# A CIN and MLP tower on one core: the 320-wide sum over d as two matmuls on 64 rows each, into two PSUM banks

## The chip, the cores and the metric

The kernel runs on one core of a Trainium2 chip. The metric is the device time of one execution in microseconds (us), as the median of several runs. One further execution was taken by the hardware profiler, and all rows below come from it.

## What is computed

For 1024 samples, 39 embedding rows of 16 numbers are gathered from 39 tables, giving `e` (sample b, field f, component d). Three cross layers follow, and then a three-layer MLP:

```python
x0 = xk = e                                   # (b, 39, 16)
for W in (f0, f1, f2):
    z = einsum('bfd,bgd->bfgd', x0, xk).reshape(b, f * g, d)
    xk = einsum('bpd,pm->bmd', z, W)          # (b, 128, 16)
    outs.append(xk)
z = concatenate(outs, axis=1).sum(-1)         # sum over d: (b, 384)
h = relu(concatenate([z, dense_ctx], 1) @ W_top1 + b_top1)
y = relu(h @ W_top2 + b_top2) @ W_top3
```

Since only the sum over d of the third layer is wanted, the kernel never forms it for each d. It forms, for each sample, field f and channel g, the sum over d of x0[f, d] * x2[g, d], called s3, and then multiplies it by f2.

## The kernel before

All arithmetic is fp32; where it matters, a product is split by hand into a high and a low part (fp32r) and made in three matmul passes. A batch is 128 samples (8 batches), a batch has 4 groups of 512 columns (32 samples times 16 values of d), and a group has 4 tiles of 128 columns, which are 8 samples times 16 values of d. A tile is a step `u`: 16 steps per batch. Each engine has its own program of the same loop: two steps ahead, then a hardware loop over batches with `u` from 2 to 17, then the last batch and a tail. Nothing but this hand-written order and the semaphores sets the order of the work.

**One step on TensorE** (`step`, `cin2`). For the second layer, a step goes through 10 banks `q` of four fields each (the last has three). For each bank TensorE makes three passes of 512 columns (lines 456, 457, 460) into one of a ring of five PSUM banks, 0 to 4. ScalarE (line 664, banks 0, 3, 5, 7) and VectorE (line 809, the other six banks) multiply each field's 128 columns by the tile's scalars x0 and add into `terms`; GpSimd adds the terms up (lines 351, 355) into `x2`, which holds the 128 columns of the tile two steps back in its partitions and 128 channels as columns.

**The sum over d** (`sum_s3`, line 470). In bank position `q == 5` (`S3_AT`) of each step from `u = 2`, TensorE multiplies `x2` as the stationary operand by `x0_diag`, a block-diagonal matrix of 8 samples times 40 columns (39 fields and a column of ones), which is 320 columns, into PSUM bank 5. ScalarE's `store_s3` (line 676) copies these to `s3` at bank position 6. There are 128 such sums. `x0_diag` is filled by eight DMAs for each group (`move_diag`), one for each sample's 16 rows; its zeros and ones are set once, in the prologue of VectorE.

**The rest of the PSUM.** Bank 6 (`X1_BANK`) takes the first layer's sum. Bank 7 (`MISC_BANK`) is shared in time by the turned scalars (`turn_scalars`, line 416: four transposes of 39x39, in tile 1 at bank position 0), the turned inputs of the next batch (`turn`, line 404, four transposes at each of four places `TURNS`, each stored by ScalarE's `store_cols`, line 616), and the third layer's matmuls `cin3` (line 480), stored by `store_r`.

**The first layer** (`cin1`, line 435). It is interleaved into tiles 1, 2 and 3 at the seven places `CIN1`; the first, in tile 1 at bank position 6, waits for the group's products, which VectorE makes (line 781) in tiles 0 and 1.

**The tail.** The last two sums, then the MLP in fp32: `layer1` (line 545), which begins each of its banks with a matmul of 16 rows (`wt1_dense`), `layer2` (555), `cin3` (480), `layer3` (562).

Of the kernel before, what the change touches and what calls it, by code (L numbers as in the profile page):

```python
# [33 lines left out]
P = 128  # L34
B, F, D, G = 1024, 39, 16, 128
# [3 lines left out]
TILES = 4  # L39
# [21 lines left out]
CHAINS = 2  # L61
TERMS = NA * FB
W1_CHUNKS = 3
S3_BANK, X1_BANK, MISC_BANK = 5, 6, 7
SPLIT = (0, 1, 2)
NS = len(SPLIT)
CIN1_ORDER = (0, 1, 3, 4, 5, 6, 2)
# [7 lines left out]
CIN1 = ((1, 6), (1, 9), (2, 2), (2, 5), (2, 8), (3, 1), (3, 4))  # L75
STORE_X1, SPLIT_X1 = (3, 4), (3, 5)
CIN3 = (7, 8, 9)
L1_BANKS = ((6, 0, 1, 2), (3, 4, 0, 1))
L2_BANKS = ((6, 2), (3, 4))
L3_BANKS = (5, 2)  # L80

ROWS_AT = (9, 3)
TURNS = ((9, 7), (10, 0), (10, 4), (10, 8))
TREE = (8, 4, 2)

def layout_constants():

    mask = (np.arange(P)[:, None] // D == np.arange(TB)[None, :]).astype(np.float32)
    return mask, np.eye(P, dtype=np.float32)  # L90

# [8 lines left out]
def cin_tower(nc, dense_ctx, ids, tables, w_top1, b_top1, w_top2, b_top2, w_top3,  # L101
              w0_pair, w0_mirror, f1, f2, c_mask, c_eye, out):
    with ExitStack() as ctx:
# [10 lines left out]
        w0 = sb("w0", [KR, KT, G])  # L114
        w0_high = sb("w0_high", [KR, NS, G], F32R)
        w0_low = sb("w0_low", [KR, NS, G], F32R)
        mask = sb("mask", [P, TB])
        eye = sb("eye", [P, P])
        ids_now = sb("ids_now", [P, F], U32)
        x0_in = sb("x0_in", [P, F, D])  # L120
# [6 lines left out]
        x1_high = sb("x1_high", [P, 2, GCOLS], F32R)  # L127
        x1_low = sb("x1_low", [P, 2, GCOLS], F32R)
        x0_scal = sb("x0_scal", [P, 2, TILES, F])
        x0_diag = sb("x0_diag", [P, 2, TILES, TB, FX])  # L130
        terms = sb("terms", [P, 2, TERMS, G])
        x2 = sb("x2", [P, 2, G])
        s3 = sb("s3", [P, FX, BATCH])
# [112 lines left out]
        @block.sync  # L246
        def _(sp):
            sp.dma_start(ids_now[:, :], ids[0:BATCH, :].bitcast(U32)).then_inc(s_ids, 16)
            sp.dma_start(w0_a.rearrange("r (k m) -> r k m", m=G), w0_pair.rearrange("k r m -> r k m")) \
                .then_inc(s_w0, 16)  # L250
            sp.dma_start(w0_b.rearrange("r (k m) -> r k m", m=G), w0_mirror.rearrange("k r m -> r k m")) \
                .then_inc(s_w0, 16)
            f1_v = f1.rearrange("(f g) m -> g f m", g=G)
            n = F // W1_CHUNKS
            for c in range(W1_CHUNKS):
                sp.dma_start(w1_raw[:, c * n * G:(c + 1) * n * G].rearrange("p (f m) -> p f m", m=G),
                             f1_v[:, c * n:(c + 1) * n, :]).then_inc(s_w1[c], 16)
            sp.dma_start(w2[:, :, :], f2.rearrange("(f g) m -> g f m", g=G)).then_inc(s_w2, 16)

            def load_ids(bt):  # L260
                sp.wait_ge(s_gather, bt * (16 * F))
                sp.dma_start(ids_now[:, :], ids[bass.ds(bt * BATCH, BATCH), :].bitcast(U32)) \
                    .then_inc(s_ids, 16)

            def move_first(j):

                at = j % GROUPS * GCOLS
                for i in range(SPT):
                    row = -KT * i % F
                    sp.dma_start(x0_first[i * F:(i + 1) * F, j % 2, :], x0_cols[row:row + F, at:at + GCOLS]) \  # L270
                        .then_inc(s_first[j % 2], 16)

            def move_diag(gf, j):

                sp.wait_ge(s_scal, gf + 1)
                sp.wait_ge(s_s3, gf * TILES - TILES + CREDIT_S3)
                for b in range(TB):
                    rows = slice(b * D, (b + 1) * D)
                    sp.dma_start(x0_diag[rows, j % 2, :, b, 0:F], x0_scal[rows, j % 2, :, :]) \
                        .then_inc(s_diag[j % 2], 16)  # L280

            def move(gf, j):

                if j > 0:

                    sp.wait_ge(s_x1, gf)
                if j % GROUPS == 0:
                    move_first(j)
                at = j % GROUPS * GCOLS  # L290
                for k in range(1, KT):
                    sp.dma_start(prods[0:KR, k, :], x0_cols[k:k + KR, at:at + GCOLS]).then_inc(s_second[k - 1], 16)
                if j == 0:
                    sp.wait_ge(s_cols, 4)
                if j % GROUPS < GROUPS - 1:
                    move_first(j + 1)

            load_ids(1)
            sp.wait_ge(s_cols, 1)
            move(0, 0)  # L300
            sp.wait_ge(s_ones, 1)
            sp.wait_ge(s_scal, 1)
            for b in range(TB):
                rows = slice(b * D, (b + 1) * D)
                sp.dma_start(x0_diag[rows, 0, :, b, 0:F], x0_scal[rows, 0, :, :]).then_inc(s_diag[0], 16)
            with sp.Fori(0, NBATCH - 2) as bt:
                for j in range(1, GROUPS):
                    move(bt * GROUPS + j, j)
                    move_diag(bt * GROUPS + j, j)
                load_ids(bt + 2)  # L310
                move(bt * GROUPS + GROUPS, GROUPS)
                move_diag(bt * GROUPS + GROUPS, GROUPS)
            for gf in range((NBATCH - 2) * GROUPS + 1, NGROUP):
                move(gf, gf % GROUPS or GROUPS)
                move_diag(gf, gf % GROUPS or GROUPS)
            for h in range(2):
                sp.wait_ge(s_oute, h + 1)
                sp.dma_start(out.rearrange("b o -> o b")[:, h * 512:(h + 1) * 512],
                             y_row[:, h * 512:(h + 1) * 512]).then_inc(s_done, 16)
            sp.wait_ge(s_done, 32)  # L320
# [67 lines left out]
        def _(pe):  # L388
            pe.sem_inc(s_s3, CREDIT_S3)

            def may_turn(bt, r):

                if r == 0:
                    pe.wait_ge(s_rows, bt * 2 + 5)
                    pe.wait_ge(s_scal, bt * GROUPS + GROUPS)
                else:
                    pe.wait_ge(s_cols, (bt + 1) * 4 + r)
# [38 lines left out]
                if k == order[-1]:  # L437
                    mm.then_inc(s_x1, 1)

            def cin2(bt, u, q, turn_next):  # L440

                n = BANKS * u + q
                old = n - RING
                if old % BANKS in ACT_BANKS:
                    pe.wait_ge(s_ya, bt * (STEPS * NA) + banks_before(ACT_BANKS, old + 1) + CREDIT_A)
                else:
                    pe.wait_ge(s_mac, bt * (STEPS * MACS) + macs_before(old + 1) + CREDIT_MAC)
                if u % TILES == 0 and q == 0:
                    pe.wait_ge(s_x1h, bt * GROUPS + u // TILES + 1)
                    pe.wait_ge(s_x1l, bt * GROUPS + u // TILES + 1)  # L450
                par, at = u // TILES % 2, u % TILES * P
                width = min(FB, F - FB * q) * G
                y = ps[:, n % RING, 0:width]
                high = w1_high[:, q * FB * G:q * FB * G + width]
                low = w1_low[:, q * FB * G:q * FB * G + width]
                nc.tensor.matmul(y, x1_high[:, par, at:at + P], high, start=True, stop=False)  # L456
                nc.tensor.matmul(y, x1_high[:, par, at:at + P], low, start=False, stop=False)  # L457
                if turn_next:
                    may_turn(bt, TURNS.index((u, q)))
                nc.tensor.matmul(y, x1_low[:, par, at:at + P], high, start=False, stop=True) \  # L460
                    .then_inc(s_y, 1)

            def sum_s3(bt, u):

                pe.wait_ge(s_x2, bt * STEPS + u - 1 + CREDIT_X2)
                j, t = divmod(u - 2, TILES)
                if t == 0:
                    pe.wait_ge(s_diag[j % 2], (bt * (GROUPS // 2) + j // 2 + 1) * (16 * TB))
                pe.wait_ge(s_s3e, bt * STEPS + u - 2 + CREDIT_S3E)
                nc.tensor.matmul(ps[:, S3_BANK, 0:TB * FX], x2[:, u % 2, :],  # L470
                                 x0_diag[:, j % 2, t].rearrange("p b f -> p (b f)"),
                                 start=True, stop=True).then_inc(s_s3, 1)

            def cin3(bt, lo, hi, scalars=NGROUP):

# [34 lines left out]
            def step(bt, u, last):  # L510
# [3 lines left out]
                for q in range(BANKS):  # L514
                    turns = not last and (u, q) in TURNS
                    if (tile, q) == SCALARS and j == 2:
                        pe.wait_ge(s_r, bt * 2 + CREDIT_R)
                    cin2(bt, u, q, turns)
                    if q == S3_AT and u >= 2:
                        sum_s3(bt, u)  # L520
                    if turns:
                        turn(TURNS.index((u, q)), MISC_BANK)
                    if front and (tile, q) == SCALARS:
# [40 lines left out]
                mm.then_inc(s_out, 1)  # L564

            def tail(bt):
                sum_s3(bt, STEPS)

                pe.wait_ge(s_r1, NGROUP)
                layer1(0)  # L570
                sum_s3(bt, STEPS + 1)
                layer2(0)
                cin3(bt, 0, F)
                layer3(0)
# [9 lines left out]
        def _(act):  # L584
# [85 lines left out]
            def store_s3(bt, u):  # L670

                if u == 2:
                    act.wait_ge(s_r, bt * 2 + CREDIT_R)
                act.wait_ge(s_s3, bt * STEPS + u - 1 + CREDIT_S3)
                at = (u - 2) * TB
                nc.scalar.activation(s3[:, :, at:at + TB],
                                     ps[:, S3_BANK, 0:TB * FX].rearrange("p (b f) -> p f b", f=FX),
                                     ACT.Copy).then_inc(s_s3e, 1)

            def store_r(bt):  # L680
# [89 lines left out]
        def _(dve):  # L770
# [41 lines left out]
            def prologue():  # L812
# [1 line left out]
                nc.vector.memset(diag[:, :, :, :], 0.0).then_inc(s_zero, 1)  # L814
                dve.wait_ge(s_zero, 1)
                dve.wait_ge(s_const, 16 * 2)
                nc.vector.tensor_copy(diag[:, :, :, F], mask[:, :].unsqueeze(1).to_broadcast([P, 2 * TILES, TB])) \
                    .then_inc(s_ones, 1)

                dve.wait_ge(s_w0, 32)  # L820
# [72 lines left out]
```

## Time and profile before

| | |
|---|---|
| median of 3 runs | 1400.6 us (1400.31 to 1401.37) |
| the profiled execution, its own time | 1401.89 us |
| its span in the profile | 1400.1 us |
| TensorE matmul busy | 1297.8 us, 93% |
| TensorE weight loads busy | 982.7 us, 70% |
| VectorE busy | 981.8 us, 70% |
| ScalarE busy | 773.4 us, 55% |
| GpSimd busy | 1040.9 us, 74% |
| granted TensorE clock, mean | 0.999 |

PE is TensorE's matmuls and PEld its weight loads, which overlap the matmuls before them; DVE is VectorE, ACT ScalarE, POOL GpSimd. Matmuls are pipelined: a row's duration holds the time in the pipe too, so successive rows overlap, and what a pass takes from the engine is read from the distance between the starts of successive rows. The chain that ended last is followed back from the last instruction, at each step to what released it. Times in rows of the timeline are counted from the start of the span.

### The profile page before, as it was taken

The numbers are of one execution on the slowest core, as the hardware profiler recorded it, in microseconds if no ns is written. First come the engines' busy times: TensorE is split into PE (matmuls) and PEld (weight loads), VectorE is DVE, ScalarE is ACT, GpSimd is POOL, SyncE is SP. The second block draws the span as 40 slices with busy tenths as digits, with TensorE's granted clock in tenths as the row PEclk, the third lists the DMA queues.
The fourth block names the chain that finished last, engine by engine and source line by source line (L and its number), as shares of the span: only waits on it lengthen the run. The fifth ranks groups of instructions, "written<-read, shape, count | busy, mean of one in ns | idle before, by whom it ended". The sixth has DMA issues, their size and how long they took to land.

```text
span 1400.1 us, 25243 instructions
## 1 busy us (share of the span) xinstructions
PE 1297.8 (93%) x5629; PEld 982.7 (70%) x5629; DVE 981.8 (70%) x3243; ACT 773.4 (55%) x2449; POOL 1040.9 (74%) x921
## 2 busy tenths in 40 slices
PE   0199999999999999999999999999999999999999
PEld 0167677876787777777777777777778777777754
DVE  2078778586877878587876878688786878688720
ACT  2146666356646665467655566466664576456631
POOL 7668888686887878788886888788786866566530
PEclk9999999999999999999999999999999999999999
DMA  8122121110211121011211112111211101111000
GB/s 218 36 82 55 47 59 53 37 43 24 59 54 51 46 59 53 5 53 46 60 53 51 46 33 58 28 53 46 60 52 52 46 12 55 45 51 45 1 1 0
DMA packets 72379, 67.51 MB, mean 48 GB/s; under 512 B 32140, under 2 KB 44402, under 8 KB 72260
## 3 DMA queue, kind: packets, MB, share of 16 engines
q1 hardware_dynamic: 59556, 62.38, 15.0%
q0 software_dynamic: 9984, 2.58, 1.9%
q10 hardware_dynamic: 2720, 1.48, 0.4%
q14 instruction: 107, 0.88, 0.2%
q8 instruction: 12, 0.20, 0.1%
HBM read 10.15 MB, written 0.00 MB: 7 GB/s over the span
## 4 chain that ended last, share of the span: by engine, by line
PE 65%; DVE 15%; issue 10%; POOL 5%; ACT 2%; DMA 1%; DVEq 1%; SPq 0%; ACTq 0%; POOLq 0%
PE ps L456 13%; PE ps L460 13%; PE ps L457 13%; PE ps L435 13%; DVE terms L809 10%; PE ps L480 5%; DVE prods L781 4%; POOL x_in L328 3%; PE ps L470 3%; PE ps L545 2%; ACT terms L664 2%; PE ps L404 2%; POOL terms L351 2%; PE ps L555 1%; DVEq L808 1%
## 5 line engine op out<-in xcount | busy, mean ns | idle before, releaser
L809 DVE SCALAR_TENSOR_TENSOR terms<-ps,x_scal,terms 128x128 f32<-128x128 f32 x2944 | 814.8, 344 | 294.2 <-PE ps L460 182.6
L664 ACT ACTIVATE terms<-ps,x_scal 128x128 f32<-128x128 f32 x2048 | 586.1, 375 | 388.9 <-PE ps L460 359.8
L351 POOL TENSOR_TENSOR terms<-terms 128x1024 f32<-128x1024 f32 (+2 forms) x384 | 565.6, 1473 | 173.7 <-DVE terms L809 152.9
L456 PE MATMUL ps<-w_high,x_high 128*128 128x512 f32 (+1 forms) x1280 | 581.6, 454 | 3.8 <-ACT terms L664 1.7
L460 PE MATMUL ps<-w_high,x_low 128*128 128x512 f32 (+1 forms) x1280 | 498.7, 390 | 1.1 <-ACT x_rows L607 1.1
L457 PE MATMUL ps<-w_low,x_high 128*128 128x512 f32 (+1 forms) x1280 | 498.3, 389 | 0.0
L328 POOL DMA_INDIRECT x_in<-in_tbl,ids_now x312 | 299.8, 961 | 97.7 <-issue 86.1
L456 PEld LDWEIGHTS ps<-w_high,x_high 128*128 128x128 f32 x1280 | 240.9, 188 | 97.1 <-DVE terms L809 21.7
L457 PEld LDWEIGHTS ps<-w_low,x_high 128*128 128x128 f32 x1280 | 241.6, 189 | 73.5 <-issue 29.8
L460 PEld LDWEIGHTS ps<-w_high,x_low 128*128 128x128 f32 x1280 | 240.9, 188 | 54.5 <-ACT x_rows L607 2.0
L435 PE MATMUL ps<-prods,w 117*128 117x512 f32 x262 | 135.3, 602 | 5.0 <-DVE prods L781 5.0
L781 DVE TENSOR_TENSOR prods<-prods,ps 117x512 f32<-117x512 f32 x192 | 130.4, 679 | 2.3 <-DMA prods<-x_cols 2.3
L219 POOL TENSOR_TENSOR prods_low<-prods,prods_high 117x512 fp32r<-117x512 f32 x93 | 119.0, 1296 | 16.4 <-DMA ids_now<-in_ids 8.6
L470 PE MATMUL ps<-x_diag,x 128*128 128x320 f32 x256 | 89.5, 431 | 0.0
L648 ACT ACTIVATE prods_high<-prods 117x512 fp32r<-117x512 f32 x93 | 60.5, 651 | 42.7 <-DVE prods L781 42.7
L480 PEld LDWEIGHTS ps<-s,w 128*128 128x128 f32 x624 | 73.1, 192 | 2.4 <-issue 0.5
L480 PE MATMUL ps<-s,w 128*128 128x128 f32 x624 | 73.2, 275 | 0.0
L355 POOL TENSOR_TENSOR x<-terms 128x128 f32<-128x128 f32 x128 | 58.9, 460 | 17.8 <-POOL terms L351 14.5
L435 PE MATMUL ps<-prods_high,w_high 117*128 117x512 f32 x93 | 39.8, 428 | 33.2 <-DVE prods L781 30.5
L404 PE MATMUL ps<-eye,x_rows 128*123 128x128 f32 x128 | 29.1, 360 | 39.3 <-ACT x_rows L704 39.3
L435 PEld LDWEIGHTS ps<-prods,w 117*128 117x128 f32 x262 | 50.0, 193 | 22.1 <-issue 7.6
L404 PEld LDWEIGHTS ps<-eye,x_rows 128*123 128x123 f32 x128 | 30.0, 299 | 41.0 <-issue 39.8
(49 smaller groups left out, 525.7 us busy)
## 6 DMA issues: line engine op xcount, KB each, us to landing
prods<-x_cols SPq DMA_DIRECT2D x192, 234.0 KB
x_first<-x_cols SPq DMA_DIRECT2D x96, 78.0 KB
x_in<-in_tbl,ids_now POOLq DMA_INDIRECT x312
x_diag<-x_scal SPq DMA_DIRECT2D x256, 9.8 KB
s<-in_f SPq DMA_DIRECT2D x3, 832.0 KB, 13.3
wt<-in_W_top ACTq DMA_DIRECT2D x1, 768.0 KB, 8.1
wt<-in_W_top ACTq DMA_DIRECT2D x1, 512.0 KB, 9.3
terms<-in_w_pair SPq DMA_DIRECT2D x1, 409.5 KB
```

Source lines behind the costliest of these rows:

```text
L219: eng.tensor_tensor(prods_low[:, i, :], prods[0:KR, SPLIT[i], :], prods_high[:, i, :].bitcast(F32), ALU.subtract).then_inc(low_ready(gf, i ...
L328: pool.indirect_dma_start(out=x0_in[:, f, :], out_offset=None, in_=tables[f], in_offset=bass.IndirectOffsetOnAxis(ap=ids_now[:, f:f + 1], ...
L351: nc.gpsimd.tensor_tensor(t[:, 0:n], t[:, 0:n], t[:, n:2 * n], ALU.add).then_inc(s_tree, 1)
L435: mm = nc.tensor.matmul(ps[:, X1_BANK, :], w, x, start=(k == order[0] and n == 0), stop=(k == order[-1] and n == len(passes) - 1))
L456: nc.tensor.matmul(y, x1_high[:, par, at:at + P], high, start=True, stop=False)
L457: nc.tensor.matmul(y, x1_high[:, par, at:at + P], low, start=False, stop=False)
L460: nc.tensor.matmul(y, x1_low[:, par, at:at + P], high, start=False, stop=True) \
L470: nc.tensor.matmul(ps[:, S3_BANK, 0:TB * FX], x2[:, u % 2, :], x0_diag[:, j % 2, t].rearrange("p b f -> p (b f)"), start=True, stop=True). ...
L480: mm = nc.tensor.matmul(ps[:, MISC_BANK, 0:BATCH], w2[:, f, :], s3[:, f, :], start=(f == 0), stop=(f == F - 1))
L664: op = nc.scalar.activation(terms[:, u % 2, FB * ACT_BANKS.index(q) + i, :], ps[:, (BANKS * u + q) % RING, i * G:(i + 1) * G], ACT.Copy, s ...
L781: nc.vector.tensor_tensor(prods[0:KR, k, :], second, ps[0:KR, bank, :], ALU.mult) \
L809: nc.vector.scalar_tensor_tensor(out=acc, in0=y, scalar=x0, in1=acc, op0=ALU.mult, op1=ALU.add).then_inc(s_mac, 1)
```

## The change

The 128 rows of the sum are cut in two halves of 64 rows (4 samples each). Each half is a matmul of its own with 160 columns, the first into PSUM bank 6 and the second into bank 7; the second alone raises the semaphore. `x0_diag` is halved to 4 samples' columns. The first layer's bank becomes bank 5. Bank 7 is now both the second half's bank and `MISC_BANK`, so waits are added on both sides: `s3_stored` before the transposes (`may_turn` and the scalars' turn), and in `sum_s3` waits for what else uses bank 7. The third of the four turns moves from bank position 4 of step 10 to position 2. ScalarE's copy reads both banks in one instruction.

```diff
-S3_BANK, X1_BANK, MISC_BANK = 5, 6, 7
+X1_BANK = 5
+S3_BANKS = (6, 7)
+MISC_BANK = S3_BANKS[1]
+HALF, HB = P // 2, TB // 2
...
-L1_BANKS = ((6, 0, 1, 2), (3, 4, 0, 1))
-L2_BANKS = ((6, 2), (3, 4))
-L3_BANKS = (5, 2)
+L1_BANKS = ((5, 0, 1, 2), (3, 4, 0, 1))
+L2_BANKS = ((5, 2), (3, 4))
+L3_BANKS = (6, 2)
...
-TURNS = ((9, 7), (10, 0), (10, 4), (10, 8))
+TURNS = ((9, 7), (10, 0), (10, 2), (10, 8))
...
-    mask = (np.arange(P)[:, None] // D == np.arange(TB)[None, :]).astype(np.float32)
+    mask = (np.arange(P)[:, None] // D % HB == np.arange(HB)[None, :]).astype(np.float32)
...
-        x0_diag = sb("x0_diag", [P, 2, TILES, TB, FX])
+        x0_diag = sb("x0_diag", [P, 2, TILES, HB, FX])
...
-                    sp.dma_start(x0_diag[rows, j % 2, :, b, 0:F], x0_scal[rows, j % 2, :, :]) \
+                    sp.dma_start(x0_diag[rows, j % 2, :, b % HB, 0:F], x0_scal[rows, j % 2, :, :]) \
...
+            def s3_stored(bt, u):
+
+                pe.wait_ge(s_s3e, bt * STEPS + u - 1 + CREDIT_S3E)
+
             def may_turn(bt, r):
 
 
+                u, q = TURNS[r]
+                s3_stored(bt, u if q > S3_AT else u - 1)
                 if r == 0:
...
                 if turn_next:
                     may_turn(bt, TURNS.index((u, q)))
+                if scalars_next:
+                    s3_stored(bt, u - 1)
                 nc.tensor.matmul(y, x1_low[:, par, at:at + P], high, start=False, stop=True) \
                     .then_inc(s_y, 1)
...
-            def sum_s3(bt, u):
+            def sum_s3(bt, u, last, front):
...
                 pe.wait_ge(s_s3e, bt * STEPS + u - 2 + CREDIT_S3E)
-                nc.tensor.matmul(ps[:, S3_BANK, 0:TB * FX], x2[:, u % 2, :],
-                                 x0_diag[:, j % 2, t].rearrange("p b f -> p (b f)"),
-                                 start=True, stop=True).then_inc(s_s3, 1)
+                if u == 2:
+                    pe.wait_ge(s_r, bt * 2 + CREDIT_R)
+                if not last:
+                    stored = sum((v, q) < (u, S3_AT) for v, q in TURNS)
+                    if u in (10, 11):
+                        pe.wait_ge(s_cols, bt * 4 + 4 + stored)
+                if front and u % TILES == SCALARS[0]:
+                    pe.wait_ge(s_scal, bt * GROUPS + u // TILES + 2)
+                for h, bank in enumerate(S3_BANKS):
+                    rows = slice(h * HALF, (h + 1) * HALF)
+                    mm = nc.tensor.matmul(ps[:, bank, 0:HB * FX], x2[rows, u % 2, :],
+                                          x0_diag[rows, j % 2, t].rearrange("p b f -> p (b f)"),
+                                          start=True, stop=True)
+                mm.then_inc(s_s3, 1)
...
-                nc.scalar.activation(s3[:, :, at:at + TB],
-                                     ps[:, S3_BANK, 0:TB * FX].rearrange("p (b f) -> p f b", f=FX),
+                nc.scalar.activation(s3[:, :, at:at + TB].rearrange("p f (h b) -> p f h b", h=2),
+                                     ps[:, S3_BANKS[0]:S3_BANKS[1] + 1, 0:HB * FX].rearrange("p h (b f) -> p f h b", f=FX),
                                      ACT.Copy).then_inc(s_s3e, 1)
```

## Rows read from the trace of the kernel before

**Rows 1.** The chain that ended last, shares of the span by engine and line

```profile
by line: PE ps L456 13.3%; PE ps L460 13.2%; PE ps L457 13.0%; PE ps L435 12.9%; DVE terms L809 10.3%; issue 10.1%; PE ps L480 5.0%; DVE prods L781 4.5%; POOL x_in L328 3.4%; PE ps L470 2.7%; PE ps L545 2.2%; ACT terms L664 1.9%; PE ps L404
```

**Rows 2.** Pieces of that chain, 600 to 637 us: start, us, what

```profile
601.82 0.17 DVE terms L809
...
613.16 0.69 DVE prods L781
613.98 0.95 PE ps L435 x3
...
622.60 0.54 PE ps L470 x2
...
633.25 0.54 PE ps L470 x2
```

**Rows 3.** Matmuls in order of time, 621.5 to 624.5 us: start, duration, engine, line

```profile
622.21 0.39 PE L460 MATMUL ps<-w_high,x_low 128*128 128x512 f32 x1
622.44 0.70 PE L470 MATMUL ps<-x_diag,x 128*128 128x320 f32 x2
622.98 1.02 PE L435 MATMUL ps<-prods,w 117*128 117x512 f32 x2
```

**Rows 4.** The 39-row transposes between full passes: timeline of both queues, 606.5 to 609.5 us

```profile
607.23 0.40 PE L460 MATMUL ps<-w_high,x_low 128*128 128x512 f32 x1
607.56 0.32 PEld L416 LDWEIGHTS ps<-eye,x_cols 39*128 39x128 f32 x4 [0.36 <-issue]
607.92 0.19 PEld L456 LDWEIGHTS ps<-w_high,x_high 128*128 128x128 f32 x1
608.26 0.39 PE L457 MATMUL ps<-w_low,x_high 128*128 128x512 f32 x1
```

**Rows 5.** Weight load of the fourth of those transposes (the timeline at 607.76 us)

```profile
607.74 0.14 PEld L416 LDWEIGHTS ps<-eye,x_cols 39*128 39x128 f32 x1
```

**Rows 6.** Matmuls of the tail's first MLP layer, 1372 to 1400 us

```profile
1373.83 1.12 PE L545 MATMUL ps<-dense_t,wt_dense 16*128 16x512 f32 x2
1374.88 2.84 PE L545 MATMUL ps<-r,wt 128*128 128x512 f32 x6
1377.65 1.12 PE L545 MATMUL ps<-dense_t,wt_dense 16*128 16x512 f32 x2
```

**Rows 7.** The chain's piece of 16 fp32 passes of 512 columns, near the end

```profile
1389.19 6.87 PE ps L555 x16
```

**Rows 8.** Waits, summed: who waited for whom, us, times, longest

```profile
PE ps L435 <- DVE prods L781: 35.5, 30, 5.0
```

**Rows 9.** The first layer's first pass in tile 1, 650.83 us, and the next

```profile
650.83 0.49 PE L435 MATMUL ps<-prods_high,w_high 117*128 117x512 f32 x1 [1.05 <-DVE prods L781]
651.17 0.40 PE L435 MATMUL ps<-prods_high,w_low 117*128 117x512 f32 x1
```

**Rows 10.** The product of VectorE which that pass waited for

```profile
650.02 0.68 DVE L781 TENSOR_TENSOR prods<-prods,ps 117x512 f32<-117x512 f32 x1
```

**Rows 11.** ScalarE's second store of turned inputs, in the fourth and the fifth batch

```profile
656.92 1.08 ACT L616 ACTIVATE x_cols<-ps 123x512 f32<-123x512 f32 x1
817.68 1.09 ACT L616 ACTIVATE x_cols<-ps 123x512 f32<-123x512 f32 x1
```

**Rows 12.** The third pass of step 10's bank 2 in these batches

```profile
657.61 0.40 PE L460 MATMUL ps<-w_high,x_low 128*128 128x512 f32 x1
817.83 0.40 PE L460 MATMUL ps<-w_high,x_low 128*128 128x512 f32 x1
```

**Rows 13.** ScalarE's copy of the sum in tile 0, ahead of the 39-row transposes

```profile
606.48 0.46 ACT L676 ACTIVATE s<-ps 128x320 f32<-128x320 f32 x1
```

**Rows 14.** Groups by line: ScalarE's copies of the sum, and VectorE's clearing

```profile
L676 ACT ACTIVATE s<-ps 128x320 f32<-128x320 f32 x128 | 58.3, 456 | 0.6 <-PE ps L470 0.6
L814 DVE MEMSET x_diag<- 128x2560 f32 x1 | 2.2, 2192 | 1.5 <-PEq L881 1.5
```

More of the change, by code:

```diff
@@ L116, in cin_tower @@
         w0_low = sb("w0_low", [KR, NS, G], F32R)
-        mask = sb("mask", [P, TB])
+        mask = sb("mask", [P, HB])
         eye = sb("eye", [P, P])
@@ L304, in _ @@
                 rows = slice(b * D, (b + 1) * D)
-                sp.dma_start(x0_diag[rows, 0, :, b, 0:F], x0_scal[rows, 0, :, :]).then_inc(s_diag[0], 16)
+                sp.dma_start(x0_diag[rows, 0, :, b % HB, 0:F], x0_scal[rows, 0, :, :]).then_inc(s_diag[0], 16)
             with sp.Fori(0, NBATCH - 2) as bt:
@@ L438, in cin1, with cin2 @@
                     mm.then_inc(s_x1, 1)
-            def cin2(bt, u, q, turn_next):
+            def cin2(bt, u, q, turn_next, scalars_next):
                 n = BANKS * u + q
@@ L517, in step @@
                         pe.wait_ge(s_r, bt * 2 + CREDIT_R)
-                    cin2(bt, u, q, turns)
+                    cin2(bt, u, q, turns, front and (tile, q) == SCALARS and u > 1)
                     if q == S3_AT and u >= 2:
-                        sum_s3(bt, u)
+                        sum_s3(bt, u, last, front)
                     if turns:
@@ L566, in tail @@
             def tail(bt):
-                sum_s3(bt, STEPS)
+                sum_s3(bt, STEPS, True, False)
                 pe.wait_ge(s_r1, NGROUP)
                 layer1(0)
-                sum_s3(bt, STEPS + 1)
+                sum_s3(bt, STEPS + 1, True, False)
                 layer2(0)
@@ L816, in prologue @@
                 dve.wait_ge(s_const, 16 * 2)
-                nc.vector.tensor_copy(diag[:, :, :, F], mask[:, :].unsqueeze(1).to_broadcast([P, 2 * TILES, TB])) \
+                nc.vector.tensor_copy(diag[:, :, :, F], mask[:, :].unsqueeze(1).to_broadcast([P, 2 * TILES, HB])) \
                     .then_inc(s_ones, 1)
```

## The prediction

> **What bounds the kernel now.** I read the chain that ended last first. By line it is the three passes of the second layer on TensorE, the first layer's passes, then VectorE's `terms` [rows 1]; the sum over d holds 2.7% of it, 0.027 x 1400 = 38 us. Then the chain in order of time, over one group [rows 2]. From 601.8 to 613.8 us it runs in VectorE: in tile 0 and the first half of tile 1, which carry the seven products, VectorE is never idle and TensorE is ahead of it. From 613.98 us to the end of tile 3 it is TensorE, pass after pass. In that stretch two sums lie on it, each a piece of 0.54 us, at 622.60 and 633.25 us: tiles 2 and 3. The sums of tiles 0 and 1 are not on it. So of 4 sums in a group 2 count: 2 x 32 = 64 of 128, and 64 x 0.54 = 35 us agrees with the 38 us (the tail's two are also in it).
>
> What a sum takes is read from starts of successive matmuls [rows 3]: the sum begins at 622.44 and the next matmul at 622.98, 0.54 us. It is two fp32 passes of 320 columns, 0.27 us each; their weight loads are hidden behind the pass before.
>
> **What the change adds to a sum: the switch.** The trace has no matmul pair on two row groups, but it has narrow ones between full-height ones, twice.
> - Four transposes of 39 rows [rows 4, 5]. The full pass before them begins at 607.23; a 512-column pass takes 0.23 (622.44 - 622.21, [rows 3]), so its columns are in at 607.46. The next weight load comes only at 607.56, 0.36 us after the engine's loads had stopped, where elsewhere it comes a pass ahead. After them, the full pass of line 457 begins at 608.26, so that of line 456 began its columns at 608.03. That is 0.57 us for four transposes, whose own pace is (607.74 - 607.56)/3 = 0.06, so 0.24. Left for leaving and coming back: 0.33 us.
> - The MLP's bank, two passes of 16 rows and six of 128 [rows 6]. A bank takes 1377.65 - 1373.83 = 3.82 us; eight such fp32 passes, by a stretch without narrow ones, 8 x 6.87/16 = 3.43 [rows 7]. Left: 0.39 us.
>
> In both, the narrow weight load waits until the full pass is through, and the full weight load after it waits again. I take 0.39, since those are fp32 passes as the sum's are, and keep 0.33.
>
> On this the Trainium skill, "TensorE: Matmul & The Clock Gate", Part 3, says that matmuls in different row groups run concurrently, their starts some 4 ns apart, and keep their order. No row here shows it; by it the 0.40 holds. The skill's "TensorEngine Tiling (Array Packing)", Theoretical Speedup, gives up to 2x for a contraction of 64 rows, which would be 0.27; its Key Properties say that changing the tiling mode drains TensorE, and speak against this change. They give no figure for that; the trace's is 0.33 to 0.39.
>
> A sum then takes 0.39 + 0.40 = 0.79 us where it took 0.54: +0.25. 64 on the chain and the tail's two, whose neighbours are fp32 matmuls: 66 x 0.25 = 16.5 us.
>
> The other 62 I cost at nothing. What covers them is VectorE's stretch: TensorE waits for the last product before the first layer's first pass, 30 times, 35.5 us with one of 5.0 [rows 8], so about 1.05 each [rows 9]. Two sums ahead of that wait add 0.5, at most 0.8. Without that cover they would cost as much again.
>
> **The waits.**
> - *The turn moved from bank 4 to bank 2 of step 10.* It now comes two banks after the second turn, and waits for ScalarE's store of it (line 616), ahead of the third pass of bank 2. That store ends at 658.00 in the fourth batch [rows 11]; the pass starts at 657.61 [rows 12]. From an engine's end to the first columns of a matmul waiting for it are 0.24 us: VectorE's product ends at 650.70 [rows 10] and the pass's columns begin at 651.17 - 0.23 = 650.94 [rows 9]. So the pass would start at 658.24, 0.63 late. The same holds in 6 of the 7 batches; in the fifth the store ends at 818.77 against 817.83, 0.94 + 0.24 = 1.18 late. Tile 2 is TensorE's own stretch, so it counts: 6 x 0.63 + 1.18 = 5.0 us. The store cannot come earlier: it stands in ScalarE's queue behind a bank's scaling.
> - *Before the scalars' turn.* ScalarE's copy of tile 0's sum ends at 606.94 [rows 13]; the third pass starts at 607.23 [rows 4], 0.29 later, and 0.24 are needed. Nothing, and a slip of tenths would fall into VectorE's stretch.
> - *The other new waits* (turn 1 and 4, the inputs and scalars stored, r3 stored) are for things that end over half a us before, by their places in the queues: nothing.
> - ScalarE's copy has the same 320 elements, 456 ns, and is waited for by nobody now [rows 14]. The eight DMAs per group move the same bytes. VectorE's clearing halves, 2.2 us to about 1.1 [rows 14], in the prologue under the gathers: nothing.
>
> **The sum.** 1401.9 (the profiled execution) + 16.5 + 5.0 = 1423.4. That execution stood 1.3 above the median of the runs, so 1422.1 for the median; I say 1422.
>
> **Rivals.**
> 1. *The halves do not overlap.* Four passes in a row, 0.54, plus the switch: +0.39 each, 66 x 0.39 = 25.7, plus 5.0: 1431.3. For it: every pass in the trace begins after the one before. Chance 0.24.
> 2. *They overlap wholly*, 0.27 (the speedup of the skill's tiling page): +0.12, or +0.06 with the switch at 0.33; 66 x 0.12 + 5.0 = 12.9, 1413.5; at the lowest 1409.6. Against it: the program order. Chance 0.07.
> 3. *Faster: the switch isn't paid here.* If the first half's weights load during the full pass before, and the full weights during the second half, a sum takes 0.40: -0.14 each, 66 x 0.14 = 9.2 less, 5.0 back from the turn: 1396.4. It decides where a sum falls below 0.54 - 5.0/66 = 0.46. For it: 64 rows are half the array, so the other half is free when the first half loads. Against it: the 39-row transposes, narrower still, paid it. Chance 0.06.
> 4. *Neither switch nor overlap*: only the turn's 5.0, 1405.6. Chance 0.04.
> 5. *A new wait costs more* (the sums ahead of the first layer's pass come out of their cover, or ScalarE falls behind at the turns): over 1433. Chance 0.06.
> 6. Mixtures of 3 and 4 that cancel to within 0.2%: chance 0.05.
>
> **How the numbers follow.** My forecast has 0.48. The range reaches from the full overlap with the low switch, 1409, past the serial case, 1433; cases 3 to 6 are mostly left out. A measurement of this kernel tells about 0.2%, 2.8 us, from no change. Slower by more: forecast, 1, 2, 4 and 5, 0.89. Within: 0.05. Faster: 0.06.
>
> **What would show it.** In the profile after, from the start of a sum's first pass to the first column of the next full one some 0.79 instead of 0.54, with a gap in the weight loads before the first half and one behind the second; the second half's first pass starting with the first half's second (0.93 in all and no common start would be rival 1). TensorE's wait for VectorE's last product down from 1.05 to about 0.55. One wait of TensorE for line 616's store per batch, 0.4 to 1.2 us. A group without turns longer by 0.5, in tiles 2 and 3. I'd be wrong if the weight load of the first half stands right behind the pass before, or if that wait for products is gone.

## The result, and the profile after

The changed kernel takes 1416.9 us (1416.5 to 1418.8) against 1401.0 (1400.3 to 1402.2): 16.0 us more, ratio 1.0115, 95% interval 1.0099 to 1.0131. The forecast was 1422, with a range of 1409 to 1433; slower was right and the size was 21 instead of 16. The profiled execution has a span of 1417.0 us against 1400.1, 16.9 more; it is the slowest of the four.

Line numbers move with the change: 456, 457, 460 are now 465, 466, 471, the first layer's 435 is 444, the sum's 470 is 491, the turns' transposes 404 are 413, VectorE's products 781 are 803, ScalarE's copy of the sum 676 is 698, its store of turned inputs 616 is 638, its scaling 664 is 686. The chain of the changed kernel, by line, answers to [rows 1]:

```profile
by line: PE ps L444 13.6%; PE ps L465 13.0%; PE ps L471 12.7%; PE ps L466 12.3%; DVE terms L831 11.5%; issue 10.7%; DVE prods L803 5.0%; PE ps L502 4.9%; POOL x_in L331 3.1%; ACT terms L686 2.7%; PE ps L491 2.3%; PE ps L567 2.2%; PE ps L413
```

The sum's share fell, from 2.7% to 2.3%, while the kernel became slower. That is the trap in this view: the time in which TensorE changes its height (the number of rows that a matmul takes, 128 at full height, 64 in the changed sum) is not charged to the sum. It is seen in the timeline of matmuls and weight loads of the changed kernel, in tile 2, which answers to [rows 3]:

```profile
628.14 0.40 PE L471 MATMUL ps<-w_high,x_low 128*128 128x512 f32 x1
628.47 0.54 PE L491 MATMUL ps<-x_diag,x 64*128 64x160 f32 x4
628.94 1.12 PE L444 MATMUL ps<-prods,w 117*128 117x512 f32 x2
...
628.47 0.30 PEld L491 LDWEIGHTS ps<-x_diag,x 64*128 64x128 f32 x4 [0.36 <-issue]
628.94 0.30 PEld L444 LDWEIGHTS ps<-prods,w 117*128 117x128 f32 x2 [0.17 <-issue]
629.48 0.19 PEld L465 LDWEIGHTS ps<-w_high,x_high 128*128 128x128 f32 x1 [0.24 <-issue]
```

The last full pass has its columns in at 628.14 + 0.23 = 628.37; the first half's weight load starts at 628.47 with the same 0.36 us gap before it as ahead of the 39-row transposes [rows 4]. The next full weights load at 628.94. In the last row the second of that matmul's two passes is 0.43 long and begins with the weight load that follows, 629.48, so its first began at 629.05. The sum takes 629.05 - 628.37 = 0.68 us by these rows, against the 0.54 of [rows 3].

What fits into so short a time shows when the four passes start. These are the rows of two narrow windows of the same timeline, just before 628.70 and at 629.00; a window shows only what runs in it:

```profile
628.47 0.41 PE L491 MATMUL ps<-x_diag,x 64*128 64x160 f32 x2
...
628.71 0.30 PE L491 MATMUL ps<-x_diag,x 64*128 64x160 f32 x2
```

Two passes begin together and the other two begin together 0.24 us later. The second half runs wholly beside the first. The rows don't say which pass belongs to which half.

What that does to a group is the distance between the first layer's first passes in tile 1 of two neighbouring groups, here one without turns. First the kernel before, then the changed one:

```profile
208.81 0.50 PE L435 MATMUL ps<-prods_high,w_high 117*128 117x512 f32 x1 [1.04 <-DVE prods L781]
...
245.67 0.50 PE L435 MATMUL ps<-prods_high,w_high 117*128 117x512 f32 x1 [1.04 <-DVE prods L781]
```

```profile
209.50 0.49 PE L444 MATMUL ps<-prods_high,w_high 117*128 117x512 f32 x1 [0.79 <-DVE prods L803]
...
246.60 0.49 PE L444 MATMUL ps<-prods_high,w_high 117*128 117x512 f32 x1 [0.80 <-DVE prods L803]
```

36.86 us became 37.10: 0.24 for the two sums of tiles 2 and 3, 0.12 each. The wait for VectorE's last product, at the end of the rows, fell from 1.04 to 0.80, by the same 0.24: the sums of tiles 0 and 1 grew too, and were paid out of it.

The waits of the changed kernel for ScalarE's stores (who waited for whom, us, times, longest), and the rows of one of each kind:

```profile
PEld ps L471 <- ACT x_cols L638: 5.0, 7, 0.7
PE ps L471 <- ACT s L698: 4.0, 2, 2.1
```

```profile
663.53 0.40 PE L466 MATMUL ps<-w_low,x_high 128*128 128x512 f32 x1
664.19 0.50 PE L471 MATMUL ps<-w_high,x_low 128*128 128x512 f32 x1 [0.26 <-ACT x_cols L638]
664.52 0.90 PE L413 MATMUL ps<-eye,x_rows 128*123 128x128 f32 x4
...
331.61 1.77 ACT L627 ACTIVATE x_rows<-x_in 128x1872 f32<-128x1872 f32 x1 [2.55 <-DMA x_in<-in_tbl,ids_now]
333.45 1.12 ACT L686 ACTIVATE terms<-ps,x_scal 128x128 f32<-128x128 f32 x4
334.45 0.45 ACT L698 ACTIVATE s<-ps 128x320 f32<-128x320 f32 x1
332.65 0.40 PE L466 MATMUL ps<-w_low,x_high 128*128 128x512 f32 x1
335.17 0.47 PE L471 MATMUL ps<-w_high,x_low 128*128 128x512 f32 x1 [2.12 <-ACT s L698]
```

The first kind is the third turn, once in each of 7 batches. The pass would have begun at 663.53 + 0.23 = 663.76; its successor begins at 664.52, so it began at 664.29: 0.53 late. The second kind was not in the forecast. In two batches the gathered rows arrive late (the 2.55 us wait on a DMA), ScalarE puts them aside, scales a bank, and only then copies the sum of step 9; the turn of bank position 7 now waits for that copy, to 335.2, where the kernel before waited only for the rows. With its weight load at 332.35 that pass was some 0.9 us late; now it is 2.4 late.

At both places the clock falls, once during the wait and once just behind it. Windows of the changed kernel (length, busy time of PE, PEld, DVE, ACT, POOL with their counts, granted clock, DMA):

```profile
336.00:339.00 3.00, 3.00 (x11) 2.61 (x10) 1.11 (x5) 1.78 (x5) 2.53 (x4) 0.50 0.01 2
820.00:827.00 7.00, 5.86 (x17) 5.02 (x18) 1.90 (x7) 3.00 (x9) 5.79 (x6) 0.53 0.06 9
```

A granted 0.50 is 1.2 instead of 2.4 GHz, and the passes that follow each other at 0.23 us are 0.43 apart. The first stretch follows the 2.12 us above; the second holds a wait of 1.91 us for the same copy in the fifth batch. The kernel before isn't free of this. These are wider windows around the two places, first in the kernel before, where the waits are 0.61 and 0.54 us, then in the changed one:

```profile
328.00:342.00 14.00, 11.87 (x47) 9.22 (x46) 8.21 (x30) 8.29 (x21) 13.28 (x11) 0.88 0.06 8
814.00:834.00 20.00, 20.00 (x84) 15.46 (x83) 12.44 (x44) 12.81 (x36) 15.21 (x14) 1.00 0.02 3
...
328.00:342.00 14.00, 10.48 (x41) 8.02 (x41) 7.43 (x26) 8.05 (x22) 12.57 (x10) 0.88 0.07 9
814.00:834.00 20.00, 17.04 (x64) 12.57 (x64) 10.60 (x37) 11.05 (x28) 17.19 (x15) 0.83 0.05 7
```

A mean of 0.88 over 14 us is 14 x 0.12 / 0.5 = 3.4 us at half clock, and 0.83 over 20 us is 6.8. So the kernel before has 3.4 us at half clock and the changed one 10.2.

The sum for the profiled execution: 66 x 0.12 = 7.9, seven third turns 7 x 0.53 = 3.7, two waits in step 9 of 1.5 more each, 3.0. That leaves 2.3 of the 16.9. The 6.8 us more at half clock can cost up to 3.4, so the slower clock accounts for it by size; no run prices it alone.

### The profile page after: what moved, and what is told of

Same layout as the page of the kernel before. It is cut to its first block, busy times and chain, and to the rows that moved or that the text cites. A ratio compares the mean times of both kernels' runs of the same rounds, so it can differ in the third digit from the quotient of the medians.

```text
span 1417.0 us, 25798 instructions
## 1 busy us (share of the span) xinstructions
PE 1318.1 (93%) x5885; PEld 968.8 (68%) x5885; DVE 981.6 (69%) x3243; ACT 775.1 (55%) x2449; POOL 1038.4 (73%) x921
## 4 chain that ended last, share of the span: by engine, by line
PE 64%; DVE 17%; issue 11%; ACT 4%; POOL 3%; DVEq 1%; DMA 1%; ACTq 0%; SPq 0%; POOLq 0%
PE ps L444 14%; PE ps L465 13%; PE ps L471 13%; PE ps L466 12%; DVE terms L831 12%; DVE prods L803 5%; PE ps L502 5%; POOL x_in L331 3%; ACT terms L686 3%; PE ps L491 2%; PE ps L567 2%; PE ps L413 1%; PE ps L577 1%; DVEq L830 1%; DMA x_in<-in_tbl,ids_now 0%
## 5 line engine op out<-in xcount | busy, mean ns | idle before, releaser
L465 PE MATMUL ps<-w_high,x_high 128*128 128x512 f32 (+1 forms) x1280 | 566.9, 443 | 3.1 <-DVE x_low L809 1.5
L444 PE MATMUL ps<-prods,w 117*128 117x512 f32 x262 | 138.7, 615 | 5.0 <-DVE prods L803 5.0
L491 PEld LDWEIGHTS ps<-x_diag,x 64*128 64x128 f32 x512 | 38.5, 184 | 47.1 <-issue 47.1
L491 PE MATMUL ps<-x_diag,x 64*128 64x160 f32 x512 | 69.5, 348 | 0.0
L444 PEld LDWEIGHTS ps<-prods,w 117*128 117x128 f32 x262 | 47.1, 193 | 22.0 <-issue 13.0
```

The source lines that it names most:

```text
L444: mm = nc.tensor.matmul(ps[:, X1_BANK, :], w, x, start=(k == order[0] and n == 0), stop=(k == order[-1] and n == len(passes) - 1))
L491: mm = nc.tensor.matmul(ps[:, bank, 0:HB * FX], x2[rows, u % 2, :], x0_diag[rows, j % 2, t].rearrange("p b f -> p (b f)"), start=True, sto ...
```

## The experiments

Theory A is the one above: a sum on 64 rows is 0.39 us for changing height and two passes' time, because passes on other rows run beside them; the rest is waits. Against it: all of it is waits (B), all of it the sum (C), or no overlap at all and a cheap switch (D). In each run the kernel before was measured beside it, at 1400.9 to 1401.0 us.

**Full rows again, everything else as changed.** The sum's two matmuls read all 128 rows and the matrix has its zeros back:

```diff
...
-                    rows = slice(h * HALF, (h + 1) * HALF)
-                    mm = nc.tensor.matmul(ps[:, bank, 0:HB * FX], x2[rows, u % 2, :],
-                                          x0_diag[rows, j % 2, t].rearrange("p b f -> p (b f)"),
+                    mm = nc.tensor.matmul(ps[:, bank, 0:HB * FX], x2[:, u % 2, :],
+                                          x0_diag[:, j % 2, t, h * HB:(h + 1) * HB].rearrange("p b f -> p (b f)"),
```

> The changed kernel, its banks, waits and turns kept, but each of the two matmuls reads all 128 rows again (the matrix keeps its zeros), so that TensorE never leaves its full height. Theory A (the 16 us are the sum on 64 rows, some 0.12 more each on 66 sums, 8 us, and the new waits, 8 us): the sum takes 0.54 us again, 1409 us, 1407 to 1411. Rival B (the waits are all of it): 1417. Rival C (the sum is all of it): 1401.

1410.5 us, ratio 1.0067 (1.0053 to 1.0080). The same group as above:

```profile
209.48 0.50 PE L444 MATMUL ps<-prods_high,w_high 117*128 117x512 f32 x1 [1.05 <-DVE prods L802]
...
246.34 0.49 PE L444 MATMUL ps<-prods_high,w_high 117*128 117x512 f32 x1 [0.98 <-DVE prods L802]
```

36.86 us, as before the change. This kernel has two matmuls and two banks as the changed one has, so these cost nothing in such a group; only the number of rows does. The narrower rows cost 1416.9 - 1410.5 = 6.4 us and the waits with the clock 9.6: the loss is of two kinds, and B and C both fall.

**The third turn's place alone**, in the kernel before:

```diff
-TURNS = ((9, 7), (10, 0), (10, 4), (10, 8))
+TURNS = ((9, 7), (10, 0), (10, 2), (10, 8))
```

> The kernel before with one edit: the third turn at bank position 2 of step 10 instead of 4, nothing else. Theory A: TensorE waits for ScalarE's store of the second turn once in each of 7 batches, 0.63 us in six and 1.18 in one: 1401 + 5.0 = 1406 us, with some 0.3 us idle in front of the third pass of that bank. Rival: the wait is taken up by a later one, 1401.

1405.5 us, ratio 1.0035 (1.0021 to 1.0048), 4.6 more. The pass that waits:

```profile
657.40 0.40 PE L457 MATMUL ps<-w_low,x_high 128*128 128x512 f32 x1
658.07 0.51 PE L460 MATMUL ps<-w_high,x_low 128*128 128x512 f32 x1 [0.27 <-ACT x_cols L616]
658.41 0.90 PE L404 MATMUL ps<-eye,x_rows 128*123 128x128 f32 x4
```

It began at 658.41 - 0.23 = 658.18 instead of 657.63, 0.55 late where 0.63 was forecast. Moving one entry of a constant costs a third of a per cent.

**Both matmuls on the same rows.** The second half reads rows 0 to 63, so the sum leaves out rows 64 to 127:

```diff
-                    rows = slice(h * HALF, (h + 1) * HALF)
+                    rows = slice(0, HALF)
```

> The changed kernel, but the second matmul reads rows 0 to 63 as the first does (rows 64 to 127 are left out of the sum). Theory A (a sum is a switch of 0.39 us and two passes of 0.135, the second half's passes wholly beside the first's because they use other rows): the four passes come one after the other, 0.39 + 0.54 = 0.93 us, 66 x 0.27 = 18 us more than the changed kernel, 1435. Rival D (the passes never overlap, 0.54 in a row, and the switch is only 0.12 here): which rows are used makes no difference, 1417.

1433.8 us, ratio 1.0234 (1.0218 to 1.0249). In the timeline the four passes begin one after the other. Shown are the sum's four together, the next matmul, and then what narrow windows at 633.57, 633.67, 633.80 and 633.93 show:

```profile
633.36 0.81 PE L491 MATMUL ps<-x_diag,x 64*128 64x160 f32 x4
634.10 0.70 PE L444 MATMUL ps<-prods,w 117*128 117x512 f32 x1
...
633.36 0.40 PE L491 MATMUL ps<-x_diag,x 64*128 64x160 f32 x1
...
633.36 0.54 PE L491 MATMUL ps<-x_diag,x 64*128 64x160 f32 x2
...
633.60 0.43 PE L491 MATMUL ps<-x_diag,x 64*128 64x160 f32 x2
...
633.74 0.43 PE L491 MATMUL ps<-x_diag,x 64*128 64x160 f32 x2
```

Each narrow window holds one pass that the one before it did not. From the first weight load to the next full-height one are 634.10 - 633.36 = 0.74 us, where the changed kernel has 628.94 - 628.47 = 0.47: 0.27 more, two passes. The time per sum is (1433.8 - 1416.9)/66 = 0.26. The overlap comes from the different rows. D falls.

**One half only.** The second half's matmul is left out (rows 64 to 127 are missing from the sum), and one full matmul in the prologue writes bank 7:

```diff
-                for h, bank in enumerate(S3_BANKS):
+                for h, bank in enumerate(S3_BANKS[:1]):
...
+                pe.wait_ge(s_scal, 1)
+                nc.tensor.matmul(ps[:, MISC_BANK, :], w0[:, 0, :], prods[0:KR, 0, :], start=True, stop=True)
```

> The changed kernel without the second half's matmul (rows 64 to 127 are left out of the sum; one full matmul more in the prologue, some 0.9 us, writes bank 7). Theory A: the second half runs beside the first, so leaving it out gives nothing: 1417 to 1418 us. Rival D (no overlap, a switch of 0.12): 0.27 less on 66 sums, 1417 + 1 - 18 = 1400. The forecast's middle way (only the middle two passes overlap): 0.135 less, 1409.

1416.6 us, ratio 1.0114 (1.0099 to 1.0130), with the extra matmul in the prologue, put at some 0.9 us in the expectation. Leaving out half of the work gives at most 1416.9 + 0.9 - 1416.6 = 1.2 us in all, 0.02 for a sum:

```profile
626.83 0.54 PE L491 MATMUL ps<-x_diag,x 64*128 64x160 f32 x2
627.29 1.12 PE L444 MATMUL ps<-prods,w 117*128 117x512 f32 x2
```

0.46 us from load to load, as with both halves. This also rules out the forecast's middle way, by which 66 x 0.135 = 8.9 us would have gone.

**Third and fourth turn after the sum.**

```diff
-TURNS = ((9, 7), (10, 0), (10, 2), (10, 8))
+TURNS = ((9, 7), (10, 0), (10, 6), (10, 9))
```

> The changed kernel with the third and fourth turns after the sum of step 10, at bank positions 6 and 9 instead of 2 and 8. Theory A: the third turn no longer waits for ScalarE's store of the second, 7 x 0.62 = 4.3 us less; the two waits of step 9 for the sum's copy stay: 1412.5 us. Rival: the third turn now waits for the copy of step 10's sum as long as it did for the other store, 1417.

1414.4 us (1413.3 to 1415.5), ratio 1.0092 (1.0077 to 1.0108): 2.5 less than the changed kernel (1416.5 to 1418.8), not 4.3. Waits of TensorE for line 638 are gone from the list, and those for the sum's copy are there (4.3 us in all, 2 times). By the measured 0.53 us it should be 3.7. The two profiled executions bear that out: their spans are 1417.0 and 1413.7, 3.3 apart, and from the first layer's first pass in tile 1 of the fourth batch's third group to that of the next, a stretch that holds the third turn, are 697.62 - 657.00 = 40.62 us in the changed kernel and 696.34 - 656.20 = 40.14 here. The medians show less, by about as much as one kernel's executions differ.

**All four turns later.**

```diff
-TURNS = ((9, 7), (10, 0), (10, 2), (10, 8))
+TURNS = ((9, 9), (10, 2), (10, 6), (10, 9))
```

> The changed kernel with all four turns later: positions (9, 9), (10, 2), (10, 6), (10, 9). Theory A: besides the 4.3 us also the two long waits of step 9 (the sum's copy stands behind the late gathered rows in ScalarE's queue) and the slower clock after them go, so that only the sum's own 66 x 0.12 = 8 us are left: 1409 us. Rival: the waits come back at the new places, 1412 or more.

1408.7 us, ratio 1.0055 (1.0041 to 1.0068). Its list of waits and its clock:

```profile
PE ps L471 <- ACT s L698: 1.7, 2, 0.9
```

```profile
core 0: 1406.8 us, clock 1.000
```

With the two waits down from 2.1 us to 0.9 at most, the clock did not fall once in this execution; one of the other four had a mean of 0.996. What is left, 1408.65 - 1400.98 = 7.7 us, agrees with 66 x 0.12 = 7.9. The run with full rows gave 6.4 for the same thing, so the two splits agree to 1.3 us and no better. So the change could have cost half of what it did, and still not nothing.

**The switch alone**, in the kernel before: one column on rows 0 to 63 behind the full-height sum, unused.

```diff
+                                 start=True, stop=True)
+                nc.tensor.matmul(ps[:, S3_BANK, 400:401], x2[0:64, u % 2, :],
+                                 x0_diag[0:64, j % 2, t, 0, F:F + 1],
                                  start=True, stop=True).then_inc(s_s3, 1)
```

> The kernel before with the sum on 128 rows as it was, and behind it one more matmul of a single column on rows 0 to 63, its result unused. It has next to no columns, so it prices leaving full height and coming back. Theory A: 0.39 us and two passes of some 0.06, 66 x (0.45 to 0.51) = 30 to 34 us: 1431 to 1435. Rival D (a switch of 0.12): 66 x 0.18 to 0.24, 1413 to 1417.

1430.6 us, ratio 1.0211 (1.0195 to 1.0226): 29.6 us, 0.45 for each of 66.

```profile
631.24 0.70 PE L470 MATMUL ps<-x_diag,x 128*128 128x320 f32 x2
631.87 0.29 PEld L473 LDWEIGHTS ps<-x_diag,x 64*128 64x128 f32 x2 [0.44 <-issue]
632.18 0.30 PEld L435 LDWEIGHTS ps<-prods,w 117*128 117x128 f32 x2
```

The full sum's columns are in at 631.24 + 0.54 = 631.78, and the narrow load follows 0.09 later; the full load at 632.18 has its columns begin 0.11 later (as 629.05 follows 628.94 above), at 632.29. A matmul of one column took 0.51 us of TensorE. The group that took 36.86 us takes 247.55 - 209.70 = 37.85 here, 0.50 for each of its two sums; the 0.45 over the whole kernel is less, so a part was covered elsewhere. It also used up the cover: TensorE's wait for the last product, 35.5 us in 30 waits before [rows 8], is down to 3 waits.

**The other way: the sum at full height, moved under cover.** The measured cover of about 1 us in tiles 0 and 1 suggests putting a sum there rather than making it narrower. In the kernel before, the sum of a step with `u % 4 == 3` is made one step later, at bank position 1, with ScalarE's copy at the same position; the last batch's last one stays.

```diff
+LATE_AT = 1
...
+        def sums_at(u, last):
+            late = [] if u % TILES or u < TILES else [(u - 1, LATE_AT)]
+            now = [] if u < 2 or (u % TILES == TILES - 1 and not (last and u == STEPS - 1)) else [(u, S3_AT)]
+            return late + now
...
-                    if q == S3_AT and u >= 2:
-                        sum_s3(bt, u)
+                    for v, at in sums_at(u, last):
+                        if q == at:
+                            sum_s3(bt, v)
...
-                    if q == S3_AT + 1 and u >= 2:
-                        store_s3(bt, u)
+                    for v, at in sums_at(u, last):
+                        if q == (at if at == LATE_AT else at + 1):
+                            store_s3(bt, v)
```

> The kernel before with full-height sums; only the sum of a group's last tile is made one step later, at bank position 1 of tile 0 of the next group, where VectorE sets the pace. 31 sums of 0.54 us leave TensorE's own stretch: 1401 - 16.7 = 1384 us, if the cover holds (TensorE's wait for the last product falls from 1.05 us to about 0.5). Rival: the sum there delays what VectorE or ScalarE wait for, and nothing or half is gained, 1393 to 1401.

1387.0 us (1386.3 to 1388.0), ratio 0.9897 (0.9882 to 0.9913): faster than both kernels. The same group:

```profile
210.34 0.50 PE L441 MATMUL ps<-prods_high,w_high 117*128 117x512 f32 x1 [0.53 <-DVE prods L789]
...
246.65 0.49 PE L441 MATMUL ps<-prods_high,w_high 117*128 117x512 f32 x1 [0.52 <-DVE prods L789]
```

36.31 us instead of 36.86, the whole 0.54 of one sum, and the wait for the product is 0.52 instead of 1.04. The gain is 14.0 us, where 31 moved sums x 0.54 would be 16.7. The profiled execution shows a loss of about that size in the prologue, where the second layer began 2.2 us later. First the kernel before, then this one, each with TensorE's first long wait:

```profile
PE ps L404 <- ACT x_rows L704: 39.3, 1, 39.3
68.20 8.47 PE L435 MATMUL ps<-prods,w 117*128 117x512 f32 x14 [5.01 <-DVE prods L781]
78.17 0.47 PE L456 MATMUL ps<-w_high,x_high 128*128 128x512 f32 x1 [1.50 <-DVE x_low L787]
...
PE ps L410 <- ACT x_rows L711: 40.7, 1, 40.7
69.59 9.30 PE L441 MATMUL ps<-prods,w 117*128 117x512 f32 x14 [5.40 <-DVE prods L789]
80.39 0.47 PE L462 MATMUL ps<-w_high,x_high 128*128 128x512 f32 x1 [1.50 <-DVE x_low L795]
```

Of the 2.2 us, 1.4 were lost before the first layer began, in the wait for ScalarE's first rows, and 0.8 in the first layer's passes. Whether that belongs to the edit or to this one execution isn't shown, and neither is whether the other three lost the same. The granted clock doesn't help here: for 68 to 72 us the kernel before is given as 1.00, yet only 5 passes fall into these 4 us and 9 into the next 4, about the pace of half clock.

No run has both halves in one bank, which would have needed no shared bank and none of the new waits. The two halves' passes run at once, as shown above, and would write the same bank with nothing to order them.

## Why the prediction was right, and where it was not

*The path.* Right. 64 sums and the tail's two count, the others are covered. The group without turns grew by twice the growth of a sum, and the wait for products shrank by twice that growth too. Both signs came at half their forecast size, because a sum grew by 0.12 and not by 0.25: 0.24 instead of 0.5 for the group, and 1.04 to 0.80 instead of 1.05 to 0.55 for the wait.

*The switch, 0.39.* Right, and it was the term that decided the sign. The sum at 0.66 to 0.68 less two passes of 0.135 is 0.39 to 0.41; one column beside a full sum cost 0.45 to 0.51, two near-empty passes included. The 39-row transposes and the tail's 16-row matmuls of the kernel before had told it beforehand. The Trainium skill, "TensorEngine Tiling (Array Packing)", Key Properties, says that a change of the tiling mode drains TensorE. The trace agrees: the half's weight load comes 0.10 us after the last column of the pass before is in (628.47 against 628.37). The price of a trip, 0.39 us, is this trace's.

*The passes, 0.40.* This step failed. "The program order is first, first, second, second; so only the middle two can overlap" is wrong: the passes begin in pairs, 0.27 in all. That was rival 2, at 0.07. The Trainium skill's "TensorE: Matmul & The Clock Gate", Part 3, says that matmuls in different row groups begin some 4 ns apart; the pairs agree with it, as far as rows of 0.01 us can. It also says that matmuls keep their order, and from that I had concluded that only the middle two passes could meet. Whether the four passes were issued in another order than I took, or did not keep it, isn't shown. 66 x 0.135 = 8.9 us of the forecast were too much.

*The third turn, 5.0.* Right mechanism; 3.7 in the changed kernel and 4.6 by itself. The pass came 0.53 us late and not 0.63, and in the fifth batch of the changed kernel the wait in step 9 had already taken the place of the 1.18.

*"The other new waits: nothing."* Wrong in two batches of seven. I read their distance in one ordinary batch. Where the gathered rows are late, ScalarE's queue puts the sum's copy behind them, and the turn waits 1.5 us longer, and more time passes at half clock; together some 5 us. Two errors of opposite sign, -8.9 and +5, brought the forecast near: that 1422 was so close to 1416.9 is in part luck.

## What to carry to other kernels

One matmul cut into two of half height lost here: the second half is free, but the trip into half height and back costs 0.39 us, more than the 0.27 that the overlap gave. By these numbers it could pay where several such pairs follow each other and share one trip; no run here has that. Look for what narrow matmuls already cost in the trace before making more of them. And where an engine's work can't be made shorter, look for a stretch in which that engine waits for another: the same sum, whole and one step later, gave 14 us.

## What was not expected of the hardware

Two fp32 matmuls of two passes each, issued one after the other on rows 0 to 63 and 64 to 127, ran as two pairs of passes. And the clock fell around waits of 1.4 to 2.2 us. In the five profiles that have such waits at the two late places (the changed kernel, full rows, same rows, one half, third and fourth turn) the windows there hold 3.4 to 6.8 us at half clock at each place, during or just behind the wait. In the five whose waits there stay below 1 us (the kernel before, the third turn alone, all four turns later, the switch alone, the late sum) it fell at one place in all: the 3.4 us of the kernel before. So the longer waits always went with a fall and the short ones once; that the length of the wait is the cause is not shown, and one profile of each kernel doesn't say how often it happens.
